# A Gram matrix in one group on four tiles of TensorE, the filters' turns in fours, and a new order of the steps

## The reference

```
xn = layernorm(x)
q, k, v = silu(short_conv(xn @ W.T))          # 4 taps, 4 heads of 64
beta = sigmoid(xn @ Wb.T)
per head, with rows cut into chunks:
    A = -tril(beta * k @ k.T, -1);  T = (I - A)^-1
    u = T @ (beta * v);  w = T @ (beta * k)
    o = q @ S + tril(q @ k.T) @ (u - w @ S);  S = S + k.T @ (u - w @ S)
y = mix of fir_3(v), fir_15(v), fir_63(v), o and v by softmax gates
x1 = x + layernorm(rmsnorm(y) @ Wo.T)
out = x1 + layernorm(ffn(layernorm(x1)))      # r, k and v projections, token shift
```

## Time and profile before

| what | value |
|---|---|
| runs, median (lowest to highest) | 604.55 us (600.88 to 604.86), 3 runs |
| the profiled execution, its own time | 602.96 us |
| its span | 601.0 us |
| mean granted clock of TensorE | 0.948 of full |
| busy in the span: PE, DVE, ACT, POOL | 498.7, 455.3, 276.3, 329.6 us |

### The profile page before, as it was taken

The page is one execution under the profiler, slowest core; times in us unless marked ns, Lnnn a source line. Parts: engine busy times, 40 slices in busy tenths (PEclk is TensorE's granted clock), DMA queues, the critical chain, the costliest instruction groups (busy, mean ns, idle before and its releaser), DMA issues.

```text
span 601.0 us, 23532 instructions
## 1 busy us (share of the span) xinstructions
PE 498.7 (83%) x9580; PEld 406.1 (68%) x9580; DVE 455.3 (76%) x1177; ACT 276.3 (46%) x688; POOL 329.6 (55%) x404
## 2 busy tenths in 40 slices
PE   3788859999998867898998988999678788989663
PEld 2666747667776655777877767788657667777553
DVE  5888684558888736788898888989648878988853
ACT  5788881115444534363545436455234344443311
POOL 6976104872316804764451786626396856756522
PEclk9999988999999989898998989999789989998978
DMA  9839346799323444513454241544524442343101
GB/s 288 230 77 272 120 132 177 170 233 202 67 43 64 117 79 88 95 31 97 74 108 101 35 107 20 133 75 76 98 30 71 113 85 42 67 87 74 37 17 35
DMA packets 155705, 61.09 MB, mean 102 GB/s; under 512 B 125008, under 2 KB 147408, under 8 KB 155600
## 3 DMA queue, kind: packets, MB, share of 16 engines
q1 hardware_dynamic: 155600, 59.61, 45.1%
HBM read 40.62 MB, written 18.95 MB: 99 GB/s over the span
## 4 chain that ended last, share of the span: by engine, by line
PE 23%; DVE 21%; issue 19%; POOL 13%; SPq 13%; ACT 7%; DMA 4%; POOLq 0%; DVEq 0%; ACTq 0%
PE bank L1669 7%; PE bank L1750 4%; DVE arena L1264 3%; DVE arena L1378 3%; POOL arena L676 3%; POOL arena L623 2%; PE bank L1585 2%; POOL seq L667 2%; SPq L438 2%; POOL seq L665 2%; SPq L455 2%; DVE arena L1366 2%; DVE arena L1393 2%; SPq L405 2%; PE bank L1786 2%
## 5 line engine op out<-in xcount | busy, mean ns | idle before, releaser
L676 POOL TENSOR_TENSOR arena<-arena,neg_half 128x2 f32<-128x2 f32 (+1 forms) x64 | 62.2, 972 | 145.4 <-DVE arena L1373 61.7
L1264 DVE SCALAR_TENSOR_TENSOR arena<-bank,small,arena 128x256 f32<-128x256 f32 x192 | 90.6, 482 | 24.0 <-ACT arena L913 19.3
L594 POOL TENSOR_TENSOR seq<-seq 128x256 f32<-128x256 f32 x32 | 23.3, 727 | 74.8 <-DVE seq L1238 42.6
L913 ACT ACTIVATE arena<-bank,small 128x256 f32<-128x256 f32 x64 | 29.4, 471 | 61.9 <-PE bank L1750 61.0
L1238 DVE TENSOR_TENSOR seq<-bank,seq 128x384 f32<-128x384 f32 x64 | 35.0, 555 | 23.0 <-PE bank L1669 13.1
L1669 PE MATMUL bank<-arena 128*64 128x192 f32 x512 | 50.3, 339 | 1.4 <-ACT arena L805 1.0
L623 POOL TENSOR_TENSOR arena<-seq,powers 128x16 f32<-128x16 f32 x16 | 46.7, 2917 | 0.0
L1750 PE MATMUL bank<-arena,w_k 128*128 128x268 f32 x128 | 37.9, 447 | 9.8 <-DVE seq L1272 6.9
L1669 PEld LDWEIGHTS bank<-arena 128*64 128x64 f32 x512 | 35.2, 140 | 11.0 <-issue 5.5
L1378 DVE TENSOR_SCALAR arena<-arena 128x256 f32<-128x256 f32 x64 | 26.5, 456 | 14.7 <-POOL arena L676 14.7
L1750 PEld LDWEIGHTS bank<-arena,w_k 128*128 128x128 f32 x128 | 26.3, 216 | 15.7 <-issue 8.8
(11 more groups left out here) (174 smaller groups left out, 1366.2 us busy)
## 6 DMA issues: line engine op xcount, KB each, us to landing
arena<-v_scratch SPq DMA_DIRECT2D x64, 128.0 KB, 3.3
arena<-fl SPq DMA_DIRECT2D x32, 192.0 KB, 6.3
arena<-fms SPq DMA_DIRECT2D x32, 192.0 KB, 6.5
arena<-xnT_scratch SPq DMA_DIRECT2D x32, 134.0 KB, 3.1
gram_scratch<-arena SPq DMA_DIRECT2D x32, 128.0 KB, 2.4
arena<-x SPq DMA_DIRECT2D x32, 128.0 KB, 3.3
out<-arena SPq DMA_DIRECT2D x32, 128.0 KB
xnT_scratch<-seq SPq DMA_DIRECT2D x2, 1027.0 KB, 6.7
```

Source lines behind the costliest of these rows:

```text
L676: pool.tensor_tensor(dst, src, half8 if k == U else neg_half[:, 0:k], ALU.pow).then_inc(s[dst_sem], 1)
L913: act.activation(cv[:, t], proj_bank(m, t)[:, 0:B * (C + PAD)].rearrange("p (b t) -> p b t", b=B)[:, :, PAD:], ACT.Copy, scale=conv_w[:, 1 ...
L1264: nc.vector.scalar_tensor_tensor(cv[:, t], ps[:, :, j:j + C], conv_w[:, 1 - t // 2, t % 2, j:j + 1], cv[:, t], ALU.mult, ALU.add).then_inc ...
```

## The change

**What it does.** The Gram matrix of a chunk is made in one group of 32 matmuls of 64 columns. For each unit and each half e the keys are multiplied by the queries into bank 2 on the same half, and by themselves into a second bank on the other half, so the four matmuls of a unit use the four 64x64 tiles of PE. That second bank (`gram_bank`) is bank 3 for the leading chunks and bank 0 from chunk 7 on, which is also the bank of the first projection and of `k_turn`. Since bank 3 is taken, q0's leading projection moves into bank 0 beside k0's. One mask and one copy of 128x512 stand in place of two of 128x256. The key part lies crosswise, so its store swaps the halves. The sums of the filters get a third buffer, and their turns are issued four at a time. `k_turn` waits for the copy of the Gram matrix that uses its bank. `beta_T` moves into space of `G_low`. All order tables are new, with a fourth part, `end_step`, and chunk 8 is scanned in the chunk steps.

```diff
+SUMS = 3
...
-        fsum = carve(seq, sf, 2 * FPAIRS, P)
+        fsum = carve(seq, sf, 2 * SUMS, P)
...
-            return bank[(3, 5)[t % 2] if t >= 2 and m < FREE else t % 2]
+            return bank[5 if t == 3 and m < FREE else t % 2]
+
+        def gram_bank(m):
+
+            return bank[3 if m < FREE else 0]
...
-                sp.wait_ge(s["g_tok_0"], m + 1)
-                sp.wait_ge(s["g_tok_1"], m + 1)
+                sp.wait_ge(s["g_tok"], m + 1)
...
-                    sp.dma_start(rows, G_tok4[HH[hh], m % 2].rearrange("p u k -> p (u k)")).then_inc(
+                    sp.dma_start(rows, G_tok4[HH[1 - hh], m % 2].rearrange("p u k -> p (u k)")).then_inc(
...
-                if h >= FPAIRS:
-                    pool.wait_ge(s["fir_turn"], 2 * (h - FPAIRS) + 2)
+                if h >= SUMS:
+                    pool.wait_ge(s["fir_turn"], 2 * (h - SUMS) + 2)
...
-            def gram_out(m, g):
-
-                act.wait_ge(s[f"gram_{g}"], m + 1)
-                act.wait_ge(s[f"at_{g}"], m + 1)
+            def gram_out(m):
+
+                act.wait_ge(s["gram"], m + 1)
                 if m >= 2:
                     act.wait_ge(s["g_odd_stored" if m % 2 else "g_even_stored"], 32 * (m // 2))
-                act.activation(G_tok4[:, m % 2, grp(g), :], units(bank[2][:, :], P)[:, :, 0:C], ACT.Copy).then_inc(s[f"g_tok_{g}"], 1)
+                act.activation(G_tok4[:, m % 2], units(gram_bank(m)[:, :]), ACT.Copy).then_inc(s["g_tok"], 1)
 
...
-            def at_parts(m, g):
-
-                dve.wait_ge(s[f"gram_{g}"], m + 1)
+            def at_parts(m):
+
+                dve.wait_ge(s["gram"], m + 1)
                 if 5 <= m < RING:
                     dve.wait_ge(s["fir_mm"], TILES)
                 if m >= RING:
                     dve.wait_ge(s["omm"], m - RING + 1)
-                nc.vector.tensor_tensor(atT[slot_of(m)][:, grp(g)], units(bank[2][:, :], P)[:, :, C:P], over(up),
-                                        ALU.mult).then_inc(s[f"at_{g}"], 1)
+                nc.vector.tensor_tensor(atT[slot_of(m)], units(bank[2][:, :]), over(up, U), ALU.mult).then_inc(s["at"], 1)
...
-                if h >= 2:
-                    fir_turn(2 * (h - 2))
-                    fir_turn(2 * (h - 2) + 1)
+                if h % 2 and h >= SUMS:
+                    for q in range(2 * (h - SUMS), 2 * (h - SUMS) + 4):
+                        fir_turn(q)
...
-                pe.wait_ge(s["conv_q0"], 3 * FREE)
+                pe.wait_ge(s["g_tok"], FREE)
...
-                if m == 0 and kind == 0:
-                    pe.wait_ge(s["weights_in"], 16 * N_W)
-                    pe.wait_ge(s["fir_prod"], TILES // 2)
+                if kind == 0 or (g == 1 and m < FREE):
+                    pe.wait_ge(s["window_odd_in" if m % 2 else "window_even_in"], 32 * (m // 2 + 1))
+                    if m == 0:
+                        pe.wait_ge(s["weights_in"], 16 * N_W)
+                        pe.wait_ge(s["fir_prod"], TILES // 2)
                 if kind == 0:
-                    pe.wait_ge(s["window_odd_in" if m % 2 else "window_even_in"], 32 * (m // 2 + 1))
                     if m >= 1:
-                        pe.wait_ge(s["conv_" + KQ[g if m <= FREE else 2 + g]], 3 * m)
+                        pe.wait_ge(s["conv_q0" if g == 0 else "conv_k1" if m <= FREE else "conv_q1"], 3 * m)
                     if m > FREE:
                         pe.wait_ge(s["ssel"], m)
                     if g == 0:
                         pe.wait_ge(s["ktok"], max(m - LEAD + 1, 0))
-                elif m < FREE:
-                    pe.wait_ge(s["window_odd_in" if m % 2 else "window_even_in"], 32 * (m // 2 + 1))
-                    if m == 0:
-                        pe.wait_ge(s["weights_in"], 16 * N_W)
-                        pe.wait_ge(s["fir_prod"], TILES // 2)
-                    else:
-                        pe.wait_ge(s["conv_" + KQ[2 + g]], 3 * m)
-                        if g == 1:
-                            pe.wait_ge(s["ssel"], m)
+                elif g == 1 and m < FREE:
+                    if m >= 1:
+                        pe.wait_ge(s["conv_q1"], 3 * m)
+                        pe.wait_ge(s["ssel"], m)
                 else:
...
-                m = min(n - 1 + LEAD, N - 1)
-                pe.wait_ge(s["conv_" + ("k0" if m < FREE else "q0")], 3 * m + 3)
+                pe.wait_ge(s["g_tok"], min(n + LEAD, N))
...
-            def gram(m, g):
-
-                if m == 0 and g == 0:
+            def gram(m):
+
+                if m == 0:
                     pe.wait_ge(s["fir_prod"], TILES // 2)
-                pe.wait_ge(s["silu_" + KQ[g]], m + 1)
-                pe.wait_ge(s["silu_" + KQ[2 + g]], m + 1)
-                pe.wait_ge(s[f"g_tok_{1 - g}"], m + g)
-                for u in range(G4):
-                    for q in HH:
-                        last = mm(bank[2][q, P * u:P * u + P], kq[slot_of(m)][q, G4 * g + u, 0, :],
-                                  kq[slot_of(m)][q, G4 * g + u], start=True, stop=True)
-                last.then_inc(s[f"gram_{g}"], 1)
+                for x in KQ:
+                    pe.wait_ge(s["silu_" + x], m + 1)
+                pe.wait_ge(s["at"], m)
+                pe.wait_ge(s["g_tok"], m)
+                for u in range(U):
+                    for e in range(2):
+                        keys = kq[slot_of(m)][HH[e], u, 0, :]
+                        mm(bank[2][HH[e], C * u:C * u + C], keys, kq[slot_of(m)][HH[e], u, 1, :], start=True, stop=True)
+                        last = mm(gram_bank(m)[HH[1 - e], C * u:C * u + C], keys, keys, start=True, stop=True)
+                last.then_inc(s["gram"], 1)
...
-            for n in range(-225, 23):
+            for n in range(-220, 44):
                 lead_step(n)
                 chunk_step(n)
                 tail_step(n)
+                end_step(n)
```

753 lines of the change are left out of this document (445 added, 308 removed).

## The result

The changed kernel takes 616.22 us (median of 4 runs, 612.72 to 617.95) against 604.7 in the same comparison: 1.020 times the time before, 95% interval 1.015 to 1.025. It is slower; 576 was forecast, with a range of 564 to 594. The profiled execution has a span of 614.2. The same program was timed again in two later sessions: 611.59 (1.016, 1.012 to 1.019) and, with additions that left no instruction in the record, 612.13 (1.014, 1.006 to 1.022).

The account below looks back on a forecast made before the run. DVE was taken to bound the seven intervals, PE close behind, and engine-hopping chains the last steps. -9.7 - 6.7 - 8.9 - 2.1 - 1.0 = -28.4 gave a span of 572.6; adding 1.96 and 1.59 gave 576, range 564 to 594.

Parts of the forecast that it names:

- Seven intervals: Chunk steps with projections, u_out of chunk 0 to 7: 171.0 becomes 164.3, -6.7, bounds +5 to -10.
- it is covered: Seven intervals: PE's chain of 3.7 after the last silu hides behind about 5 of DVE work, some 0.8 to spare.
- DVE's 22.2 of work keeps its size: Seven intervals: DVE's work, some 22.2 of a quiet interval of 23.48, stays as it was.
- The wait of 0.79 goes: Seven intervals: DVE's 0.79 wait for the first convolution's tap vanishes, as k0's projection now precedes scan_so.
- rival C: Gram matrix: tiles don't run side by side, it costs 2.18 as before; total 584, chance 0.05.
- The start: Everything up to u_out of chunk 0: 228.7 becomes about 219, -9.7, bounds -3 to -12.
- the -3: Start: filters' turns in fours save 0.28 per two pairs over 22 pairs before the first leading projection.
- Rival A: SP's in-order queue returns the solve late; only -4 of the start and -3 of the transition remain: 588, chance 0.22.
- (4): Start, from the first solve to u_out of chunk 0: 23.0 shortened by new PE order and earlier return; u_out about 219.
- Transition: Two intervals, u_out of chunk 7 to 9: 50.3 becomes 41.4, -8.9, bounds 0 to -11.
- Last steps and end: Six last steps -2.1 (-0.35 each, one POOL wait less; bounds +3 and -6); end -1 (bounds 0 and -3).
- rival D: PE left idle, its clock falls in most steps and lengthens the chain: 612, slower than before, chance 0.04.

Follow-up runs that it names:

- e9: The changed kernel with the sums of squares made by 16 products of 64 stationary columns instead of 32 of 32: 601.55 us (0.997).
- e1: The changed kernel with POOL's direct part made after the last power in the chunk steps: 620.34 us (1.029).
- second profile: The profile of the changed kernel itself, unaltered, run once more in a later comparison: 611.59 us (1.016).
- e14: e12 with POOL's direct part made after the power for the first norm, clear of the solve: 603.72 us (1.001).
- e12: e9 with PE waiting on 3 semaphores instead of 6 in front of the Gram matrix: 599.02 us (0.994).
- e11: e9 with the Gram matrix in 16 products of 128 columns over two tiles, with two masks and two copies: 609.24 us (1.011).
- e7: The kernel before with only the filters' turns in fours and three buffers for sums: 602.74 us (0.999).
- e13: e12 with SP's early return of the first solve and, in the end steps, the last mixing ahead of the statistics: 596.89 us (0.989).
- e15: e13 with SP fetching the diagonal of chunk 3 in front of the blocks: 599.15 us (0.993).
- e2: The changed kernel with the key mixing behind the output's norm and ffn_k behind off_first: 621.46 us (1.033).

## Why the prediction was wrong

**Seven intervals (-6.7 forecast, +9 measured).** The step that failed is this one: "gram 1.16, off_second 0.7, sumsq 0.7, scan_kq 1.16 ... that is 3.7, and DVE has about 5", so "it is covered". Each group went in with the duration it has where instructions are there. In the step shown, from the Gram matrix (349.3) to the end of scan_kq (about 354.7) it was 5.4, the difference being the piece of 1.58, and k_turn and scan_u behind it took 3.8 instead of the 2.3 of e9's profile at full clock. And the chain was not covered: DVE waited for scan_kq in front of `rest_in` in all seven intervals, 6.2 us in total, where before it never did; with the short sums it was 2.2. Six to seven us of the miss are gone when 64 instructions a chunk are (e9: 180.0 to 173.6). A second premise failed beside it, "DVE's 22.2 of work keeps its size": DVE was busy for 144.9 us of the seven intervals before and 150.2 after, and e1, where the mixing pair runs clear of POOL's direct part, has 145.0. "The wait of 0.79 goes" failed too: k0's projection stands in front of scan_so, but behind scan_u, and DVE waits for its tap for 11.2 us in the seven intervals (9.5 in the second profile), 8.7 before. Of the remaining 9 (173.6 against 164.3) the 5.3 of DVE's work and the 0.66 in front of the Gram matrix may be parts; e1, e14 and e12 could not turn them into time, so their shares are not settled.

**The Gram matrix.** Right: 1.16, and rival C fell (all four tiles work side by side). The leading step without a torn group is 9.7 (145.53 to 155.20), better than the 10.2 I gave. Its price as C put it, half of 16 x 1.0, is near what e11 against e9 measured, 7.7, though that measurement reaches from 4 to 13. What was missing is its other side, twice the instructions.

**The start (-9.7 forecast, +1.3 and -5.4 measured).** The filters' pitch was right, 3.34 for two pairs instead of 3.64, but the -3 was not: in e7, which has this part alone, the first leading projection came 1.0 earlier, and in the changed kernel at 134.7 and 134.1 instead of 133.0, with PE waiting up to 0.85 for the filters' loads. In the earlier trace rows I read "1.84 <-issue" as PE standing at the first correction for its own reasons, and counted 1.8 of gain when the correction would be passed early. It was the very mechanism that decided the case, at a block's end by its number, and stood in a row I quoted. Rival A, the queue of SP, was also at work: the solve ended at 204.8 and its store was issued at 210.62, 5.9 held where I had 2.4. But in e13 and e15 its removal alone gave nothing. The second profile, with no torn group in its leading steps, divides the miss best: there the solve ended at 200.1, earlier than the 201.3 I gave, and the way from it to u_out took 23.2, as before the change (23.0), where I had 17.7. So the part that failed is (4), the way from the solve to u_out. Its terms, put together, give 219.7 and not 219.

**Transition (-8.9 forecast, +2.2 measured).** I took chunk 9's interval as 18.5; it was 26.6. PE waits 3.74 for the first correction of chunk 9, which DVE makes behind the scaling of the last blocks and the statistics, and then runs y_rows at half clock (3.78 for 1.89) and ffn_k (2.04) ahead of scan_u. This is read from the trace; no run tried it.

**Last steps and end.** The last steps were right in the first profile (108.9 for 108.6). The end is 2.4 to 3.7 longer, of which the late mixing of chunk 15 may be 1 (e13 against e12, one profile each).

**Rivals and chances.** The case that came, slower, had 0.04, as rival D: the clock falls because PE is left idle. That is not what happened: the clock granted in the seven intervals was 0.97 and 0.99, higher than the 0.95 before, and the time was lost in idle pieces themselves. D's own bound was off as well: PE's 20.6 passes an interval of 22.9 at a mean of 0.90, not 0.82. I had no rival in which more and smaller instructions cost something by their number, and summed each part as if it had its own time.

## What to carry to other kernels

Before splitting matmuls into more and smaller ones, count instructions in a row: four for a float32 product. Where a view of waits has "issue" inside a group, number PE's rows: if the pieces stand 256 or a multiple of it apart, the supply is short there, and more such products can cost what they give; fewer, longer products (16 for 32 in the sums, though each group took 0.3 longer) gave 10 us here and 3 in the kernel before. Such pieces stand at fixed places of the program, and each edit moves those behind it: time an edit together with a version of it that is shifted by half a block, which I did not do for e9. And a piece taken out of a ring of engines can be worth nothing, as in e2, until what it covered is known.

The best version found is e13, 1.1% (0.6 to 1.6) faster than the kernel before; e15, which differs by one fetch, measured 0.7% (0.4 to 1.0), so the two can't be told apart.

## What the runs showed that I had not expected

- PE runs dry inside a group of small products, for 0.2 to 3.7 us, in both kernels, always at the end of a block of 256 instructions; 32 products at the start of the program cost 14 us, 3.7 of it by starting the rest later.
- Behind some of these pieces PE's clock is at its lower level (3.29 and 3.94 for projections of 2.07), behind others as long it is not: in the second profile it was granted in full from 235 to 439, with pieces of up to 1.86.
- With quiet queues and the clock at 0.50 PE takes 1024 rows of small products at 0.027 us each with one piece of 0.16.
- Empty instructions at the start of PE's program left the count of recorded instructions, and the places of the pieces, as they were.
- A DVE instruction on 128x8 elements takes 1.50 us instead of 0.16 beside POOL's addition on 128x512.
